# Turning the adjacency row blocks with one transposing DMA each, in a two-layer graph attention kernel

## What is computed

```
x = layernorm(x + layer0(x, adj, pairs, Wq, bq, Wk, bk))
x = layernorm(x + layer1(x, adj, W_seq, a1, a2, W_out, b_out))
```

```
scores = zeros.at[:, sub, obj].set(att); masked by adj; diagonal = 1e-7
layer0 = (softmax(scores).sum(heads) / 8) @ x
```

## Time and profile before

| | |
|---|---|
| median of 3 runs | 456.04 us (455.86 to 457.72) |
| the profiled execution: time | 455.99 us |
| its span | 454.2 us |
| PE busy | 401.1 us (88%) |
| DVE busy | 359.8 us (79%) |
| POOL busy | 176.9 us (39%) |
| ACT busy | 162.8 us (36%) |
| mean granted TensorE clock | 0.958 |

### The profile page before, as it was taken

The page is one execution under the profiler, slowest core; times in us unless marked ns, Lnnn a source line. Parts: engine busy times, 40 slices in busy tenths (PEclk is TensorE's granted clock), DMA queues, the critical chain, the costliest instruction groups (busy, mean ns, idle before and its releaser), DMA issues.

```text
span 454.2 us, 5539 instructions
## 1 busy us (share of the span) xinstructions
PE 401.1 (88%) x1826; PEld 211.1 (46%) x1826; DVE 359.8 (79%) x998; ACT 162.8 (36%) x268; POOL 176.9 (39%) x184
## 2 busy tenths in 40 slices
PE   1598999998999979999898927889999999999970
PEld 1154545454554535555555524445555455554430
DVE  1999799675385778888987675999999999998573
ACT  4866846555352423433332220001122111123322
POOL 7777777775100001400000057556455556450000
PEclk9899999999999996999998976989999999999996
DMA  7998244343420228111111147547444555540162
GB/s 273 371 379 285 94 140 140 116 164 103 143 83 1 85 75 303 64 58 48 49 48 47 50 119 213 171 126 211 141 120 132 149 132 149 154 122 0 46 233 100
DMA packets 25681, 61.73 MB, mean 136 GB/s; under 512 B 7461, under 2 KB 7589, under 8 KB 23594
## 3 DMA queue, kind: packets, MB, share of 16 engines
q1 hardware_dynamic: 16554, 39.06, 23.9%
q0 software_dynamic: 9088, 22.20, 17.9%
HBM read 52.72 MB, written 8.52 MB: 135 GB/s over the span
## 4 chain that ended last, share of the span: by engine, by line
PE 56%; POOL 19%; DVE 14%; issue 7%; ACT 1%; DMA 1%; DVEq 0%; POOLq 0%; ACTq 0%
POOL avals L462 18%; PE ps L863 16%; PE ps L786 11%; PE ps L749 10%; PE ps L581 6%; PE ps L755 2%; PE ps L865 2%; DVE adjT L1743 2%; PE ps L620 2%; PE ps L741 1%; PE ps L773 1%; PE ps L788 1%; DVE stats L1567 1%; DVE stage L1730 1%; DVE arenaC L1559 1%
## 5 line engine op out<-in xcount | busy, mean ns | idle before, releaser
L553 POOL DMA_INDIRECT adjT<-seqtab,eidx x80 | 82.6, 1032 | 135.5 <-DMA seqtab<-scores 77.9
L581 PE MATMUL ps<-arenaB,adjT 128*128 128x512 f16 x512 | 117.1, 385 | 6.2 <-ACT adjT L909 3.0
L863 PE MATMUL ps<-adjT,stage 128*128 128x512 f32 x160 | 91.4, 663 | 10.8 <-DVE adjT L1743 10.8
L462 POOL DMA_INDIRECT avals<-in_adj_dram,aidx x79 | 81.6, 1033 | 24.0 <-issue 24.0
L581 PEld LDWEIGHTS ps<-arenaB,adjT 128*128 128x128 f16 x512 | 49.5, 99 | 64.9 <-ACT adjT L909 4.8
L749 PE MATMUL ps<-stage 128*128 128x512 f32 x128 | 61.4, 625 | 0.0
L786 PE MATMUL ps<-adjT 128*128 128x512 f32 x128 | 57.9, 595 | 3.2 <-ACT adjT L1015 3.2
L1743 DVE TENSOR_TENSOR adjT<-adjT 128x512 f32<-128x512 f32 x80 | 50.2, 692 | 5.6 <-ACT adjT L1059 5.6
L865 PEld LDWEIGHTS ps<-adjT,stage 128*128 128x128 f32 x160 | 31.6, 197 | 40.5 <-issue 40.5
L909 ACT COPY adjT<-ps 128x1024 f16<-128x1024 f16 x32 | 30.8, 1013 | 44.0 <-PE ps L568 44.0
L1133 DVE MAX8 arenaA<-arenaA 128x8 f16<-128x256 f16 x120 | 40.7, 411 | 0.5
(11 more groups left out here) (261 smaller groups left out, 502.9 us busy)
## 6 DMA issues: line engine op xcount, KB each, us to landing
stage<-in_adj_dram SPq DMA_DIRECT2D x16, 1024.0 KB
arenaA<-in_x_dram SPq DMA_DIRECT2D x4, 1024.0 KB, 13.2
seqtab<-arenaA SPq DMA_DIRECT2D x16, 256.0 KB, 2.0
out_dram<-arenaC SPq DMA_DIRECT2D x16, 256.0 KB, 2.6
arenaB<-in_x_dram SPq DMA_DIRECT2D x1, 1536.0 KB, 10.1
adjT<-seqtab,eidx POOLq DMA_INDIRECT x80, 3.8
avals<-in_adj_dram,aidx POOLq DMA_INDIRECT x79
arenaC<-in_L_gnn_Wq_dram SPq DMA_DIRECT2D x1, 1024.0 KB, 9.2
```

What stands on the lines that cost most here:

```text
L462: g.indirect_dma_start(out=avals[:, t:t + 1], out_offset=None, in_=adj_flat, in_offset=bass.IndirectOffsetOnAxis(ap=aidx[:, t:t + 1], axis ...
L553: g.indirect_dma_start(out=G[:, b % GR, k, :], out_offset=None, in_=seqtab, in_offset=bass.IndirectOffsetOnAxis(ap=eidx[:, b * KE + k:b * ...
L581: ins = t.matmul(bank(4 + b % 2), adjT[:, b, j, :], xsplit[:, w, j, :], start=(j == 0 and w == 0), stop=(j == NB - 1 and w == 1))
L863: t.matmul(bank(2 + b % 2), ehot[:, b % 2, k, :], G[:, b % GR, k, 0:D], start=False, stop=(k == KE - 1), skip_group_check=True)
```

## The change

The 16 transposes on PE and the two ACT copies of each block go. In their place ACT issues, behind the cast of a block, one DMA that turns the whole block of 128 x 2048 f16 (512 KB), from `arowh` to `adjT[:, b]`. `multiply(b)` and the cast of block b + 2 wait for this DMA. The PSUM banks of the turned blocks are no longer used, and `pair_rows` loses its wait for them. The load of x for the normalization (L390) waits for all turning DMAs. `wa_made` is waited for ahead of the DMA of block 12.

```diff
@@ SP
-            sp.wait_ge(row_turned, 2 * NB)
+            for k in range(2):
+                sp.wait_ge(row_turned[k], 8 * NB)
@@ PE
-            def turn_rows(b):
-                pe.wait_ge(row_cast, b + 1)
-                if b >= 2:
-                    pe.wait_ge(row_evac, 2 * (b - 1))
-                for j in range(NB):
-                    ins = t.transpose(turn_banks(b)[:, j, :], arowh[:, b % 2, j * P:(j + 1) * P], identh[:])
-                    if j % 8 == 7:
-                        ins.then_inc(row_turned, 1)
             def multiply(b, lo, hi):
                 if lo == 0:
-                    pe.wait_ge(row_evac, 2 * (b + 1))
+                    pe.wait_ge(row_turned[b % 2], 16 * (b // 2 + 1))
             def pair_rows():
-                pe.wait_ge(row_evac, 2 * (NB - 1))
                 pe.wait_ge(diag_made, 1)
-            turn_rows(0)
             for b in range(NB):
 ...
                     multiply(b, 0, NB // 2)
-                    turn_rows(b + 1)
@@ ACT
             def cast_row(b):
                 act.wait_ge(c_row[b % 2], 16 * (b // 2 + 1))
                 if b >= 2:
-                    act.wait_ge(row_turned, 2 * (b - 1))
+                    act.wait_ge(row_turned[b % 2], 16 * (b // 2))
                     act.wait_ge(row_listed, b - 1)
-            def save_turned(b):
-                for k in range(2):
-                    act.wait_ge(row_turned, 2 * b + k + 1)
-                    s.copy(adjT[:, b, 8 * k:8 * k + 8, :], turn_banks(b)[:, 8 * k:8 * k + 8, :]).then_inc(row_evac, 1)
+            def turn_row(b):
+                act.wait_ge(row_cast, b + 1)
+                if b == 12:
+                    act.wait_ge(wa_made, 2)
+                act.dma_start_transpose(adjT[:, b], arowh[:, b % 2, :]).then_inc(row_turned[b % 2], 16)
             cast_row(0)
+            turn_row(0)
             for q in range(4):
 ...
-                if q == 0:
-                    save_turned(0)
                 if q == 1:
                     cast_row(1)
-            save_turned(1)
+                    turn_row(1)
             cast_row(2)
+            turn_row(2)
             def block_step(b):
                 if b + 1 < NB:
                     cast_row(b + 1)
+                    turn_row(b + 1)
 ...
-                if b == 12:
-                    act.wait_ge(wa_made, 2)
-                save_turned(b)
                 save_ax(b - 2)
```

More of the change, by code:

```diff
@@ L196, in two_layer_graph_attention @@
         w_turned, w_evac_d, w_evac_a = sem("w_turned"), sem("w_evac_d"), sem("w_evac_a")
-        row_cast, row_turned, row_evac, row_listed = (sem(n) for n in ("row_cast", "row_turned", "row_evac", "row_listed"))
+        row_cast, row_listed = sem("row_cast"), sem("row_listed")
+        row_turned = [sem("row_turned0"), sem("row_turned1")]
         ax_made, ax_saved = sem("ax_made"), sem("ax_saved")
@@ L293, in x_again @@
             return x_soon[:, b, :] if b < 4 else x_late[:, b, :]
-        def turn_banks(b):
-            k = 2 * (b % 2)
-            return ps[:, k:k + 2, :].rearrange("p a c -> p (a c)").bitcast(F16).rearrange("p (j i) -> p j i", j=NB)
         seq = part(arenaA, 0, [NB, D])
```

## The result

The kernel with the turning DMAs takes 487.31 us (median of 4 runs, 482.90 to 492.47) against 455.95 us for the one before (4 runs beside it, 455.5 to 457.72): a ratio of 1.0664, 95% interval 1.0619 to 1.0709. It is slower, and the time lies 9 us above the predicted range. All ratios here leave out executions that took over 1.5% more than the fastest of their kernel, as the one of 492.47 us. The profiled execution took 482.9 us and spans 481.2 us, the lowest of its four times; before, the span was 454.2.

A forecast was written before the change was run, and what follows sets the result against it. POOL's gathers bound the kernel to 112 us, PE from 114 to 166 us. Transposes gone from the path, -3.56, plus lowered clock, +2.5, give -1.1 us on 455.99: 454.9 us; own range 454.0 to 456.0, wider 452.2 to 478.

The forecast's parts named there:

- The bound of the kernel before: Up to 112 us POOL's 79 gathers bound the chain; from 114 to 166 us PE itself, blocks 11 to 15.
- 3.56 - 2.5 = 1.1: Transposes of blocks 12 to 15 leave PE's path, 3.56 us; lowered clock behind L599's wait hands back 2.5.
- The half clock: PE, after idling 13 us instead of 2.09 at L599, runs at clock 0.50, losing 2.1 to 3.0 us, 2.5 taken.
- D: ACT's time issuing one turning DMA, in which it does nothing else; hidden up to 4.4 us, not from 5 on.
- T: Transfer time of one block's turning DMA; 3 us taken, between 1.5 and 11.3, hidden to about 8.6 us.
- a start bound by x's low parts as before: At the start, without transposes of blocks 2 and 3, block 3's matmuls begin at about 44.7 us instead of 49.10.
- ACT's issue is the bound: Rival, chance 0.28: with D over 4.4 us, saved products and PE step at 2.5 + D; at 6.9 us, 478 us.
- the slow transfer: Rival, chance 0.11: turns at 11.3 us one after another, block 15 multiplied at 197 instead of 166; about 487 us.
- the estimate of 20.9 us a block: Transfer of one block by the skill page's 1309 ns per 128 x 128 turn, if 16 pieces did not overlap.
- The issue estimated from "DMA: Bandwidth & Descriptors": Issue of one turn by an older generation's sequencer table: 4,096 cycles, 3.4 us at 1.2 GHz; forecast would stand narrowly.
- The signs named for "wrong": PE waiting for L913 or the turn every block, unreleased ACT gaps behind L900, DVE waiting for L900, L599 late.
- The warning that POOL's gathers could suffer: Sign at PE's wait L599: if itself late, POOL's gathers suffer from turns on the shared DMA engines.

The follow-up runs named there:

- number 1: Changed kernel plus turns behind its last store, alone, back to back and beside SP's row loads: alone a turn lands after 4.3 us, beside four loads 15.3.
- number 6 by ACT: Against the kernel before: TensorE still turns blocks 0 to 2, ACT-issued DMAs turn the rest; 465.71 us, ratio 1.0154.

## Why the prediction was wrong

- **The bound of the kernel before: right.** Without any turning the gain was 3.0 us in the time and 2.5 us at the normalization; forecast were 3.56 - 2.5 = 1.1. The pause was 10.8 us instead of 13. The half clock cost 2.0 us instead of the 2.5 taken, and 0.9 us came from an earlier last gather, which no term of the sum had. By "TensorE: Matmul & The Clock Gate" of the Trainium skill (Part 1) the low clock is the default, and the trace agrees at this second place.
- **The failed step: the two costs of the added DMAs, D and T, both taken as hidden.** The prediction had "Up to 4.4 us D is hidden", took D to be below that, took T as 3 us, and let block 3 start at "about 44.7 us" with "a start bound by x's low parts as before". Block 3 started at 74.67 us, 30.0 us later. Blocks 3 to 10 took 67.04 us instead of eight times 6.91, 11.7 us more. Of these 41.7 us the 13.8 us of forecast idle time before the count took up their part, and 27.95 us were left. The steady part alone would have fitted: 44.7 + 67.04 = 111.7 us, ahead of 113.8. So it was the start that failed, where D was 12.21, 5.95 and 13.14 us for turns 1 to 3 and the landing took 22 to 23 us for turns 0 and 2.
- **D.** It was 5.46 us in the median, with two of 12 and 13 us and one of 9.6. My reasoning bounded it by the issue of a plain load on an idle queue, 0.43 us, and took it for a property of the instruction. It is 1.3 to 1.9 us alone and mostly 5.3 to 6.7 us beside a row load, whose length it takes on. In the kernel there is always such a load, since the row cast frees the buffer that SP then fills while ACT issues the turn. The threshold of 4.4 us was not tested by itself: no kernel had ACT issue beside the loads with a D near it.
- **The rival "ACT's issue is the bound" is what happened in the steady blocks**, with its formula (a step of 2.5 + D) right: 8.00 us measured at D = 5.45. At the start the other rival, the slow transfer, was true beside it. Its price, 478 us at a constant 6.9 us, was 9 us short, although the mean D was lower (5.5 us): it had no late first turn, and no lowered clock or late x rows behind the count. That 487.31 us is the 487 us of the slow transfer's rival is luck: it had every turn at 11.3 us, and in the steady blocks PE waited for none. The first rival deserved more than 0.28: I had no row for D between 0.43 and 15 us, and a cost unknown over that range, with a limit of 4.4, spoke for at least an even chance.
- **T = 3 us: right alone, wrong beside loads.** 2.5 to 2.6 us of transfer alone; 7.9 us to the landing beside one load, 15.3 beside four. I bounded T by 89 ns as a price for a turn's own packet; at the start the sum has to add the packet of the neighbour to one's own, 88 + 19 ns. The first turn took from 9.14 to about 32 us. The earlier trace rows was also misread: the 524 packets of 123 to 128 us are the load of weights for layer 1. A row load is as large but goes in 144 packets, with a share of 3.5 us of the 16 engines instead of 2.9. And (114 - 9) / 12 is 8.75 us, not 8.6. Neither slip decides.
- **The rules of the Trainium skill.** "VectorE: DVE Perf Modes" (The three transpose paths) gives 1309 ns for a 128 x 128 piece. Here 16 pieces landed in 4.3 us alone, 0.27 us each, and in 15.3 us beside four loads, 0.96 each, so the estimate of 20.9 us a block was too long. The page's rule (Rules for kernel authors) to leave such turns to TensorE where the result may stand in PSUM is borne out with ACT issuing (31 us lost), and not with SP issuing: all turns by DMA can't be told from before (0.998), and the blocks from 3 on by DMA are slightly better (0.9953). The issue estimated from "DMA: Bandwidth & Descriptors", 3.4 us, lay above the 1.3 to 1.9 us measured alone and below the 5.5 us beside a load.
- **The signs named for "wrong"** were the ones seen: ACT gaps behind no releaser at L900, DVE waiting 29.2 us for the cast. The warning that POOL's gathers could suffer did not come true for the 79 entries (the last is issued at 109.5 us, before at 109.19) and did for the x rows.
- **Where the forecast did apply:** with SP issuing and TensorE turning the first three blocks, the count is at 113.81 us (forecast 113.8 within 0.3), PE's wait 10.1 us (8 or more), the normalization at 165.5 (166), the time -2.2 us (-1.1).

## What to carry to other kernels

Before a DMA's issue is put on a compute engine's queue, ask what stands behind it there and what DMA traffic stands beside it: an issue with thousands of small packets isn't over until part of it has moved, and that part can stand behind another queue's load. The first ones, beside the loads of the start, are the dearest. Put it on a queue whose owner has nothing urgent, if possible the one that carries the competing loads, so that they go one behind the other. And a saving ahead of a wait for something else only makes the wait longer, with a lowered clock to pay behind it as here (2.0 us).

## What the runs showed of the hardware

- Where two queues both have packets on the DMA engines, they alternate packet by packet, not byte by byte: 476 of 2 KB beside 479 of 256 bytes in 3 us, and 158 of some 7 KB beside 158. Beside a single row load issued with it, a turn sent nothing for 3 us (93 packets and none, 78 to 81 us) and followed behind it; no run tested why. Nor does a turn's packet always take 19 ns: in 48 to 58 us of the changed kernel 1,106 of them took 54.9% of the 16 engines, 79 ns each, and what slowed them is open.
- The issue of a transposing DMA of 512 KB takes 1.3 to 1.9 us alone, and mostly 5.3 to 6.7 us beside a 1 MB load of another queue. At its end about a quarter of the turn's 2,080 packets had moved: 542 in the tail of number 1 alone, 560 there beside a load, 602, 539, 546, 555 and 546 in the changed kernel (the issues at 77.39, 85.39, 93.42, 118.16 and 126.02). The exception there is the issue at 148.07, beside the load of weights in 2 KB packets: 4.75 us and 158 packets.
- Every fourth issue on ACT's queue was short, also beside a load, with hardly a packet moved by its end. In the changed kernel these are turns 4, 8 and 12 (1.34, 1.33, 1.33 us; none, 3 and none of their packets moved); with TensorE turning the first three blocks, the 5th, 9th and 13th DMA (1.33, 1.33, 1.38); in the tail of number 1 the 21st and the 29th, the second beside a load, where it landed 7.5 us later all the same. The issue that follows a short one within 6 us is the longest of its four: 9.63 and 6.68 us in the changed kernel, 10.92, 10.83 and 14.18 us in number 6 by ACT. In these 2,524, 2,496, 2,375, 2,548 and 2,575 packets moved, all of the turn ahead and some 300 to 500 of its own. That suggests a ring of descriptors in which a turn finds room at once only every fourth time; no run tested it, and it stays open. On SP's queue, which carries the loads too, the pattern is not seen.
- Turns alone move some 210 GB/s (2,080 packets of 256 bytes in 2.5 us).
